# Blocks of keys that begin one key later, a router one group earlier, and one mask matmul per score unit

## What is computed

```python
h = tok(x)                                    # running averages both ways, then a 128 -> 256 projection
h = h + attn0(layernorm(h))                   # one head of 256, rotary, mask = tril(k=1)
h = h + ffn0(layernorm(h))                    # dense path + sparse path
h = h + attn1(layernorm(h))                   # 16 heads, local window of 128 keys
h = h + ffn1(layernorm(h))                    # quantised linear layers
```

## Time and profile before

| | |
|---|---|
| median of 3 runs | 1842.0 us (1836.56 to 1849.58) |
| profiled execution | 1843.25 us, its span 1841.5 us |
| mean granted PE clock in the profile | 0.874 of full speed (2.4 GHz) |
| stage a | 0 to 289 us |
| stage b | 289 to about 880 us |
| stage c | about 905 to 1340 us |
| stage d | 1343 to 1729 us |
| stage e | to 1841 us |

### The profile page before, as it was taken

One profiled execution on the slowest core, in us unless ns is written; L12 is line 12 of the kernel. 1 busy time (PEld: TensorE's weight loads), 2 busy tenths in 40 slices (PEclk: granted clock), 3 DMA queues, 4 the chain that ended last, 5 costly groups with the idle time before them and its releaser, 6 DMA issues. The chain is left out here.

```text
span 1841.5 us, 31980 instructions
## 1 busy us (share of the span) xinstructions
PE 1477.5 (80%) x10890; PEld 1168.6 (63%) x10890; DVE 1134.6 (62%) x2510; ACT 700.7 (38%) x1429; POOL 284.3 (15%) x217
## 2 busy tenths in 40 slices
PE   4677886978886977889498999788677988889765
PEld 4567775656654645655387888677565766767535
DVE  5676654765774675773464443467566675767596
ACT  1122230443543434345253553343223423233385
POOL 1111110311200301310000001752202220100000
PEclk8788996897898978879798999899788989889987
DMA  4000034134124216212341333320346342141001
GB/s 128 1 1 1 0 101 102 36 102 103 45 74 127 62 35 177 60 57 71 124 134 51 104 101 101 98 68 12 103 121 197 87 138 66 57 120 27 2 3 68
DMA packets 102602, 141.19 MB, mean 77 GB/s; under 512 B 30467, under 2 KB 91372, under 8 KB 102444
## 3 DMA queue, kind: packets, MB, share of 16 engines
q1 hardware_dynamic: 85644, 120.67, 22.7%
q0 software_dynamic: 12672, 13.45, 2.8%
q10 hardware_dynamic: 4134, 5.13, 1.0%
HBM read 77.27 MB, written 61.27 MB: 75 GB/s over the span
## 5 line engine op out<-in xcount | busy, mean ns | idle before, releaser
L1507 DVE TENSOR_REDUCE b_neg<-b_ps 125x1 f32<-125x500 f32 (+3 forms) x304 | 183.4, 645 | 109.3 <-PE b_ps L1085 98.9
L1257 ACT ACTIVATE b_probs<-b_ps 125x500 f32<-125x500 f32 (+1 forms) x352 | 187.8, 568 | 150.7 <-PE b_ps L1120 133.7
L1079 PE MATMUL b_ps<-b_k_st,b_q_st 96*125 96x500 bf16 (+3 forms) x512 | 155.0, 348 | 55.5 <-DMA b_k_st<-scratch_stacks 43.5
L1257 ACT ACTIVATE d_probs<-d_ps 125x504 f32<-125x504 f32 (+1 forms) x176 | 100.3, 588 | 171.6 <-PE d_ps L1120 153.5
L1116 PE MATMUL b_ps<-b_q_st,b_k_st 99*125 99x500 bf16 (+3 forms) x512 | 148.2, 342 | 16.1 <-ACT b_probs L1257 12.5
L1507 DVE TENSOR_REDUCE d_neg<-d_ps 125x2 f32<-125x504 f32 (+2 forms) x176 | 115.2, 678 | 52.4 <-PE d_ps L1082 46.7
L1079 PEld LDWEIGHTS b_ps<-b_k_st,b_q_st 96*125 96x125 bf16 x512 | 76.4, 154 | 95.1 <-DMA b_k_st<-scratch_stacks 44.4
L1079 PE MATMUL d_ps<-d_k_st,d_q_st 96*125 96x252 bf16 (+2 forms) x384 | 100.5, 295 | 26.4 <-DMA d_k_st<-scratch_stacks 16.7
L1116 PE MATMUL d_ps<-d_q_st,d_k_st 99*125 99x252 bf16 (+2 forms) x384 | 94.3, 281 | 22.2 <-ACT d_probs L1257 13.0
L180 PE MATMUL c_ps<-c_hd,c_dw_hi 128*128 128x500 f32 x192 | 79.5, 414 | 36.7 <-DVE c_ag L2177 25.2
L1116 PEld LDWEIGHTS b_ps<-b_q_st,b_k_st 99*125 99x125 bf16 x512 | 70.3, 149 | 57.6 <-ACT b_probs L1257 40.3
(11 more groups left out here) (384 smaller groups left out, 4028.5 us busy)
## 6 DMA issues: line engine op xcount, KB each, us to landing
scratch_stacks<-b_part SPq DMA_DIRECT2D x48, 375.0 KB, 4.7
scratch_stacks<-d_part SPq DMA_DIRECT2D x48, 375.0 KB, 4.5
b_q_st<-scratch_stacks SPq DMA_DIRECT2D x16, 562.5 KB, 5.4
b_k_st<-scratch_stacks SPq DMA_DIRECT2D x16, 562.5 KB, 6.9
d_q_st<-scratch_stacks SPq DMA_DIRECT2D x16, 562.5 KB, 5.0
d_k_st<-scratch_stacks SPq DMA_DIRECT2D x16, 562.5 KB, 6.5
c_xrows<-scratch_slots SPq DMA_DIRECT2D x54, 128.0 KB, 2.1
c_ew_raw<-in_L_ffn_ew_dram SPq DMA_DIRECT2D x24, 256.0 KB, 5.5
```

The lines of the kernel that those rows point to most:

```text
L1079: mm = pe.matmul(out, q_st[0:STACK, hh, i * TT:(i + 1) * TT], k_st[0:STACK, hh, k0:k0 + n], start=True, stop=True)
L1257: act.activation(dst, second_out(x, unit), ACT.Exp).then_inc(c["exp"].sem, 1)
L1507: dve.tensor_reduce(dst, ps[:TT, bank, 0:per * n].rearrange("p (m n) -> p m n", n=n), AX_X, ALU.max, negate=True).then_inc(free_sem(t, p), 1)
```

## The change

1. `width(i)` becomes 125 (i + 1) + 1, and the blocks `keys(j)` begin one key late: 0 to 125 (126 keys), then 126 to 250, ..., the last of 124. So tile `i` needs `i + 1` blocks. Tiles that held 125 partitions hold `KT` = 126, and DVE fills four banks of PSUM with zeros once before its first scaling of weights. The wait of the scores for the split queries and keys covers two halves less for width 376 (a half's width).
2. The three router steps move to `FRONT_AT + 1.1 - GROUPS` to `FRONT_AT + 1.3 - GROUPS`, that is -1.388, -1.338 and -1.213: for the loop's trips after the last group's `turn` of the batch before, and just ahead of the first scores of group 0.
3. In `first` and `second` the heads of a unit are all multiplied first (only the first of them starts the bank), and then one mask matmul adds the mask to all of them, with the mask repeated for each head by its access pattern and the output a view of `per` (or `nh`) pieces.

```diff
@@ -23,6 +23,7 @@
 FIRST = 1
 SEGS = ((0, BANK), (BANK, T))
 NEG = -1e30
+KT = TT + 1
 ROUND = 1.5 * 2.0 ** 23
 
 
@@ -213,14 +214,14 @@
         rot = m.sb("a_rot", [P, 2, KC, T], F32)
         qk_hi = m.sb("a_qk_hi", [P, 2, KC, T], F32R)
         qk_lo = m.sb("a_qk_lo", [P, 2, KC, T], F32R)
-        v_hi = m.sb("a_v_hi", [TT, NT, D], F32R)
-        v_lo = m.sb("a_v_lo", [TT, NT, D], F32R)
+        v_hi = m.sb("a_v_hi", [KT, NT, D], F32R)
+        v_lo = m.sb("a_v_lo", [KT, NT, D], F32R)
         neg_max = m.sb("a_neg_max", [TT, NT], F32)
         denom = m.sb("a_denom", [TT, NT], F32)
         rden = m.sb("a_rden", [TT, NT], F32)
         probs = m.sb("a_probs", [TT, 2, T], F32)
-        pT_hi = m.sb("a_pT_hi", [TT, 2, NT, TT], F32R)
-        pT_lo = m.sb("a_pT_lo", [TT, 2, NT, TT], F32R)
+        pT_hi = m.sb("a_pT_hi", [KT, 2, NT, TT], F32R)
+        pT_lo = m.sb("a_pT_lo", [KT, 2, NT, TT], F32R)
         zeros = m.sb("a_zeros", [P, D], F32)
         zeroed = Memory(nc, sems, keep).stage_sem("a_zeroed")
         ps = m.ps("a_ps", [P, 8, BANK])
@@ -277,7 +278,11 @@
 
         def width(i):
 
-            return min(T, (i + 2) * TT)
+            return min(T, (i + 1) * TT + 1)
+
+        def keys(j):
+
+            return (j * TT + 1 if j else 0), min(T, (j + 1) * TT + 1)
 
         def ahead(name, eng, kind, args, t, which):
 
@@ -373,15 +378,16 @@
                     bank = side(t, p)
                     for i in (2 * g, 2 * g + 1):
                         for kc in range(KC):
-                            mm = split3(pe, ps[:TT, bank, (i % 2) * D:(i % 2 + 1) * D],
-                                        [x[:, kc, i * TT:(i + 1) * TT] for x in (uT_hi, uT_lo)],
+                            k0, k1 = keys(i)
+                            mm = split3(pe, ps[:k1 - k0, bank, (i % 2) * D:(i % 2 + 1) * D],
+                                        [x[:, kc, k0:k1] for x in (uT_hi, uT_lo)],
                                         [w[:, 2, kc, :] for w in (w_hi, w_lo)], kc == 0, kc == KC - 1)
                     mm.then_inc(c["unit_mm"].sem, 1)
                 elif kind == "scores":
                     (i,) = args
                     if i == 0 and isinstance(t, int) and t == 0:
                         pe.wait_ge(load, REST_LOADS)
-                    pe.wait_ge(c["qk_lo"].sem, at("qk_lo", t, which, 2 if width(i) < HALF else 4))
+                    pe.wait_ge(c["qk_lo"].sem, at("qk_lo", t, which, 2 if width(i) <= HALF else 4))
                     if i >= 2 or not (isinstance(t, int) and t == 0):
                         pe.wait_ge(c["exp"].sem, at("exp", t, which, i - 1))
                     if i == 3 and isinstance(t, int) and t == B - 1:
@@ -404,19 +410,21 @@
                     (i,) = args
                     pe.wait_ge(c["exp"].sem, at("exp", t, which, i + 1))
                     pe.wait_ge(c["pT_lo"].sem, at("pT_lo", t, which, i))
-                    for j in range(width(i) // TT):
-                        mm = pe.transpose(ps[:TT, 4 + j // 4, (j % 4) * P:(j % 4) * P + TT],
-                                          probs[:, i % 2, j * TT:(j + 1) * TT], ident[:TT, :TT])
+                    for j in range(i + 1):
+                        k0, k1 = keys(j)
+                        mm = pe.transpose(ps[:k1 - k0, 4 + j // 4, (j % 4) * P:(j % 4) * P + TT],
+                                          probs[:, i % 2, k0:k1], ident[:TT, :TT])
                     mm.then_inc(c["pT_mm"].sem, 1)
                 elif kind == "weigh":
                     (i,) = args
-                    n = width(i) // TT
+                    n = i + 1
                     pe.wait_ge(c["pT_lo"].sem, at("pT_lo", t, which, i + 1))
                     pe.wait_ge(c["v_lo"].sem, at("v_lo", t, which, (n + 1) // 2))
                     bank = side(t, p)
                     for j in range(n):
-                        mm = split3(pe, ps[:TT, bank, 0:D], [x[:, i % 2, j, :] for x in (pT_hi, pT_lo)],
-                                    [x[:, j, :] for x in (v_hi, v_lo)], j == 0, j == n - 1)
+                        k0, k1 = keys(j)
+                        mm = split3(pe, ps[:TT, bank, 0:D], [x[:k1 - k0, i % 2, j, :] for x in (pT_hi, pT_lo)],
+                                    [x[:k1 - k0, j, :] for x in (v_hi, v_lo)], j == 0, j == n - 1)
                     mm.then_inc(c["unit_mm"].sem, 1)
 
             trips.run(pe, step)
@@ -452,7 +460,7 @@
                 elif kind == "v":
                     (g,) = args
                     act.wait_ge(c["unit_mm"].sem, unit_done(t, p))
-                    act.activation(v_hi[:, 2 * g:2 * g + 2, :].rearrange("p i d -> p (i d)"), ps[:TT, bank, :], ACT.Copy)\
+                    act.activation(v_hi[:, 2 * g:2 * g + 2, :].rearrange("p i d -> p (i d)"), ps[:KT, bank, :], ACT.Copy)\
                        .then_inc(c["v_hi"].sem, 1)
                 elif kind == "scores":
                     (i,) = args
@@ -466,9 +474,9 @@
                     act.wait_ge(c["pT_mm"].sem, at("pT_mm", t, which, i + 1))
                     if i >= 2 or not (isinstance(t, int) and t == 0):
                         act.wait_ge(c["h_upd"].sem, at("h_upd", t, which, i - 1))
-                    n = width(i) // TT
+                    n = i + 1
                     act.activation(pT_hi[:, i % 2, 0:n, :],
-                                   flat(4).rearrange("p (j q) -> p j q", q=P)[:TT, 0:n, 0:TT], ACT.Copy)\
+                                   flat(4).rearrange("p (j q) -> p j q", q=P)[:KT, 0:n, 0:TT], ACT.Copy)\
                        .then_inc(c["pT_hi"].sem, 1)
 
             trips.run(act, step)
@@ -514,6 +522,8 @@
             dve.wait_ge(set_const, 1)
             dve.wait_ge(load_x, 16)
             ema(-1, 1)
+            dve.memset(flat(4)[:KT], 0.0)
+            dve.memset(flat(6)[:KT], 0.0)
             dve.wait_ge(load_w, W_LOADS)
             dve.tensor_scalar(w_raw[:, 0], w_raw[:, 0], float(D) ** -0.5, None, ALU.mult).then_inc(set_scale, 1)
             dve.wait_ge(set_wT, 1)
@@ -583,7 +593,7 @@
                 elif kind == "v":
                     (g,) = args
                     dve.wait_ge(c["v_hi"].sem, at("v_hi", t, which, g + 1))
-                    dve.tensor_tensor(v_lo[:, 2 * g:2 * g + 2, :].rearrange("p i d -> p (i d)"), ps[:TT, bank, :],
+                    dve.tensor_tensor(v_lo[:, 2 * g:2 * g + 2, :].rearrange("p i d -> p (i d)"), ps[:KT, bank, :],
                                       v_hi[:, 2 * g:2 * g + 2, :].bitcast(F32).rearrange("p i d -> p (i d)"),
                                       ALU.subtract).then_inc(c["v_lo"].sem, 1)
                     dve.wait_ge(c["v_lo"].sem, at("v_lo", t, which, g + 1))
@@ -596,9 +606,9 @@
                 elif kind == "turn":
                     (i,) = args
                     dve.wait_ge(c["pT_hi"].sem, at("pT_hi", t, which, i + 1))
-                    n = width(i) // TT
+                    n = i + 1
                     dve.tensor_tensor(pT_lo[:, i % 2, 0:n, :],
-                                      flat(4).rearrange("p (j q) -> p j q", q=P)[:TT, 0:n, 0:TT],
+                                      flat(4).rearrange("p (j q) -> p j q", q=P)[:KT, 0:n, 0:TT],
                                       pT_hi[:, i % 2, 0:n, :].bitcast(F32), ALU.subtract)\
                        .then_inc(c["pT_lo"].sem, 1)
                     dve.reciprocal(rden[:, i:i + 1], denom[:, i:i + 1]).then_inc(c["rden"].sem, 1)
@@ -830,7 +840,8 @@
         steps_of_batch += over(t0, t0 + 0.30, [("qk", (n, ec, s)) for s in range(2) for ec in range(KC)])
         steps_of_batch += [(t0 + 0.33, ("cut", (n,)))]
     if not local:
-        steps_of_batch += [(-0.39, ("router", ())), (-0.385, ("route", ())), (-0.3, ("place", ())), (0.3, ("table", ()))]
+        steps_of_batch += over(FRONT_AT + 1.1 - GROUPS, FRONT_AT + 1.2 - GROUPS, [("router", ()), ("route", ())])
+        steps_of_batch += [(FRONT_AT + 1.3 - GROUPS, ("place", ())), (0.3, ("table", ()))]
     steps_of_batch += [(-4e-4 + 1e-4 * k, ("v", (k,))) for k in range(3)]
     for g in range(GROUPS):
         steps_of_batch += weigh_group(g)
@@ -1073,17 +1084,16 @@
                 if args[1] == 0:
                     pe.wait_ge(c[f"stacked{g}"].sem, at(f"stacked{g}", t, which))
                 bank = side(t, p)
+                out = ps[:TT, bank, 0:per * n].rearrange("p (k n) -> p k n", n=n)
                 for k in range(per):
                     hh = g * HG + h0 + k
-                    out = ps[:TT, bank, k * n:(k + 1) * n]
-                    mm = pe.matmul(out, q_st[0:STACK, hh, i * TT:(i + 1) * TT], k_st[0:STACK, hh, k0:k0 + n],
-                                   start=True, stop=True)
-                    if local:
-                        mm = pe.matmul(out, identb[:TT, :TT], mask_q[:, mc:mc + n], start=False, stop=True,
-                                       skip_group_check=True)
-                    elif k0 + n == (i + 1) * TT:
```

(23 more changed lines are left out.)

## The result

The changed kernel takes 1798.08 us (median of 4 runs, 1796.51 to 1799.38) against 1839.28 us for the kernel before in the same session: ratio 0.9773, 95% interval 0.9749 to 0.9797, 41 us less. 1800 was forecast, from a profiled 1843.25.

What follows compares the result with a forecast made beforehand. Neither TensorE nor VectorE alone was taken to set stage one; TensorE bounds the 16-head stage outside its hole. Terms -13 - 28 - 2 = -43 from the profiled 1843.25 us gave 1800 us; range 1784 to 1826.

Steps and rivals of the forecast that it cites:

- Part B: 16-head stage: router one group earlier, into the hole before the first scores; -28 us, ends 0 and -32.
- The three later stretches: Batches 1 to 3, router's first matmul to first matmul after its placing: 28.2 - 9.6 = 18.6 us saved.
- The fit in the hole: Batches 1 to 3: router, moved-back seconds and chain to the placing end at worst at 417 to 418, ahead of 420.50.
- The placing in front of batch 0's first score: Batch 0's first score, free to start at 296.73, is delayed 4 us by the placing, leaving 7.8 of 11.8 us.
- The clock term of 2 us: Scores right after the router gain 0.5 us a batch without its thin work lowering the granted clock before them.
- Part A: Stage one's keys one key later, blocks per batch from 26 to 21: -13 us for four batches, ends 0 and -21.
- the share: Stage one: TensorE's busy share, 73 to 79% of a batch, of its 4.3 us saving counts: 3.3 us a batch.
- Stage one goes by VectorE: Rival: in stage one the key change gives only 1 us a batch, total 1809 us; chance 13%.
- Part C: One mask matmul per unit in 16-head and windowed stages, 656 fewer matmuls with columns unchanged: -2 us, at most 5.
- the slow masks: Rival: merged masks stream slower; at half rate 1894 us, chance 7%; only outputs in pieces slow, 1810 us, 5%.
- the loads that were not hidden: Rival: the 656 removed mask matmuls' weight loads were not hidden, 70 us more gained, 1730 us; chance 2%.
- The signs: Right: stage-one batches 2 to 4.5 us shorter. Wrong: TensorE idle for the router's membership before first scores of batches 1 to 3.

Runs made afterwards that it cites:

- the first trace: Profiled execution of the changed kernel, all three parts of the diff against the kernel before: span 1796.3 us.
- e2: The kernel before with only the router, route and placing moved one group earlier: 1809.40 us, ratio 0.9839.
- e8: The changed kernel timed again, nothing altered: 1797.63 us.
- e7: The changed kernel with the placing of batch 0 alone moved behind that batch's first scores and their turn: 1796.51 us.
- e11: The changed kernel with nine mask matmuls of 500 columns, result overwritten, ahead of TensorE's wait for the membership in batch 0 alone: 1799.26 us.
- e6: The changed kernel with two products instead of three in stage one's weighing: 1799.27 us.
- e5: The changed kernel with stage one's maxima taken over the first 126 columns only, instead of 126 to 750: 1798.68 us.
- e10: The changed kernel with both stage-one reliefs, maxima over 126 columns and two products in the weighing: 1795.08 us.
- e3: The kernel before with only the merging to one mask matmul per unit: 1837.82 us, ratio 0.9998.
- e1: The kernel before with only stage one's blocks of keys one key late: 1828.73 us, ratio 0.9941.
- e4: The changed kernel with the placing six units of first scores later, in all batches: 1805.44 us, ratio 0.9814.

## Why the prediction was right, and where its terms were off

**Part B, forecast -28, measured -29.5 alone.** The three later stretches were sized as they came out: first score to first score the stage lost 12.5, 7.4 and 6.3 us, for 11.8, 6.7 and 5.2 forecast. The last batch, to stage c, lost 10.6 for 6.7, but that stretch took 184.4 to 188.1 us in three traces with the router in its old place and 177.0 to 180.7 in the first trace, e2 and e8, so a part of the 10.6 is spread. The fit in the hole, by 3 us at worst, came out as 4.7 (399.2 to 403.9). The forecast's 417 to 418 takes the chain to the placing beside the moved-back second scores; its three terms one after another, as it tells them, would give 420.7 and no room. In the trace the placing starts 10.9 us after the router's first matmul, so they do run side by side. The placing in front of batch 0's first score was forecast to cost 4 us; it cost 4.4 in the first trace (13.41 us from stage one's last matmul to the first score, before 8.96) and 2.0 to 4.5 in others, as the router's matmuls fell into either clock. The clock term of 2 us had the least ground and seems too small: in e2, without the other parts, the four stretches lost 33.9 us, 3.5 over the 30.4 of the work alone. That the clock rose where the router stood is shown by the second 20 us from batch 1's first score on, before and after:

```profile
440.50:460.50 20.00, 19.75 (x174) 16.11 (x174) 11.33 (x51) 4.84 (x12) 6.21 (x6) 0.74 0.26 65
...
423.90:443.90 20.00, 19.14 (x180) 14.46 (x181) 12.08 (x23) 10.27 (x24) 0.00 (x0) 1.00 0.23 60
```

That the 3.5 us are the clock's is argued; no run changes it alone. What the forecast called the cost of batch 0's wait is not all that stands there, though: e7 and e11 show VectorE busy 18 of 20 us behind it.

**Part A, forecast -13, measured -10.** TensorE's busy time in the four batches is 13.0 us less, for 17 forecast (4.3 us a batch: the 3.9 at full clock, divided by a granted 0.90; at the mean of 0.87 it is 4.5). The step that was off is the share: "TensorE is busy 73 to 79% of a batch ... I take that share". Busy share is not the chance that an engine is on the path. The relief of TensorE alone (e6) gave 36% of what it took away, VectorE's (e5) 15%, both together (e10) 64% of their 18 us, each by one trace and with some 3 us of spread: part A, which relieves both at once and TensorE the more, got 10 of the 21 us of its upper end. The forecast also has no term for the clock, which fell from 0.867 over stage one to between 0.837 and 0.857; how much of the missing 3 us is the clock's and how much the share's, no run separates. The rival "Stage one goes by VectorE", at -4, gave too little. The fills of PSUM cost nothing, as forecast: 0.91 us each in the trace after, and the weight scaling behind them starts without a wait.

**Part C, forecast -2, measured -1.1 with an interval of some 4 us on either side.** No more can be said than that it is small. The steps of 0.11 and 0.22 us settle the slow masks, the time of e3 the loads that were not hidden. The 107 ns that the forecast calls a mean weight load are busy time over the number of loads, which overlap; a row of one lasts 161 ns on average in the kernel before. Both are longer than the step of 0.06 us, so the argument stands.

**The sum** of 43 was off by 2 because A's excess of 3 and C's of 1 are partly cancelled by B's shortfall of 1.5, which is luck. So is some of the 1800: it starts from a profiled execution 4 us above the 1839.28 of the same session.

**The signs** that the forecast named are mixed. TensorE does wait for the membership before the first scores of batches 1 to 3, 0.7 to 0.9 us each, which was to be a sign of being wrong; it costs nothing, since the keys land later. Of the four batches of stage one, one is shorter by 2 to 4.5 us in the first trace and three in e1.

## What to carry to other kernels

Where two engines take turns, price a saving by relieving each alone and both at once: alone, either one's gain is mostly hidden. After work has been removed, look at the written-out order again, at the waits that are left: two constants gave 9 us here. A filler belongs in a hole that a transfer sets, in front of what the transfer releases, and not among the work behind it, where its stall went with a lower clock as well.

## What the runs showed of the hardware

- The same code of stage one was granted 0.76 to 0.88 in its first batch and took 58.5 to 54.0 us, the longer the lower the clock (six traces). With less work for TensorE the stage was granted less over its four batches: 0.837 to 0.857 against 0.867 to 0.868.
- VectorE's 2.3 us of placing among the reductions right after a hole went with a granted clock of 0.71 and 0.75 over 20 us in two batches of three, where 0.89 is granted without it (e4). Nine dense matmuls in a wait went with 0.67 instead of 0.50 in the 20 us after it (e11).
- A matmul that reads its moving columns once per head by its access pattern, and one that writes pieces of 125 columns 250 apart, go at the pace of plain ones (0.22 us for 504 columns, 0.11 for 250).
